# The routed expert part of a conv and mixture-of-experts block, in tiles of 128 tokens instead of 256

## The chip, the cores and the metric

The kernel runs on one NeuronCore of one Trainium2 chip. The metric is the device time in microseconds of that core, taken as the median of several runs; lower is better. One profiled execution of the same program gives the trace from which all rows below are read. In these rows PE is the matrix engine (TensorE), PEld its weight loads, PEldq its instruction sequencer, DVE is VectorE, ACT is ScalarE, POOL is GpSimd, and SP issues DMAs. PEclk is the share of TensorE's full clock that was granted: 1.00 is 2.4 GHz and 0.5 is 1.2 GHz.

## The reference

The input is 32 images of 128 channels with 32x32 pixels in float32. A dynamic depthwise 3x3 convolution runs first; after it every pixel is a token of 128 channels, 32768 in all, and each token goes through two of eight experts:

```python
x = x + _L0_conv_ref(_ln_c(x), ...)       # taps from per-channel mean and max, softmax over taps
t = _to_tokens(x)                         # (32768, 128)
# in _L0_ffn_ref, on xf = layernorm(t):
gate_logits = xf @ Wg + bg
top_w, top_i = jax.lax.top_k(gate_logits, 2)
top_w = jax.nn.softmax(top_w, axis=-1)
for e in range(8):
    h = gelu(xf @ W1[e] + b1[e])          # W1[e]: 128 x 512
    out = out + w_dense[:, e:e+1] * (h @ W2[e] + b2[e])   # W2[e]: 512 x 128
t = t + out
```

## The kernel before

The program has three stages, and every engine's order is written out by hand, with semaphores between the engines.

The **first stage** (0 to about 640 us) goes over pairs of images: layer norm, convolution, the gate, and the choice of the two experts. Its last step writes each token as a row of 133 numbers (128 channels, the two weights, the token's number, and the two numbers of its layer norm, `NMR` and `RSTD`) to DRAM by an indirect DMA of GpSimd (L439), into one of 28 lists: one list for each pair of experts. W1 and W2 are loaded into one buffer, `stage`, one after the other, and split into a high and a low float16 part (`split_weights`, L475 to L482 on ACT and L903 to L912 on DVE), which lie side by side in `wall`.

**Between the stages** DVE makes a table of the tiles (which rows, which two experts), and each list is filled up with empty rows to a whole tile (`pad`).

The **expert stage** goes over NT = 156 tiles of T = 256 rows (32768/256 = 128, and 28 for the lists' ends). For each tile SP loads the rows; ACT normalises them (`normalise`, L600); PE transposes them (`turn_rows`, L810) and ACT and DVE split the result into `xh` and `xl`. For both experts (side 0 and 1) `up` makes the hidden layer with 12 matmuls of 256 columns: four slices of the hidden layer times three products, high x high, high x low and low x high. ACT applies the gelu slice by slice, because each slice has its own bias column (L616). The result is split into `gh` and `gl`, and `down` takes the 128x128 blocks of these as the stationary operand and the weights as the moving one: `gh` against the high and the low weights at once (`both`, 256 columns, L841), `gl` against the high ones (128 columns, L842), and two matmuls for the bias (L845). DVE weighs the results (`combine`), GpSimd adds the two halves and the token's input (L447, L449) and scatters the rows to DRAM (L454).

Which expert a tile belongs to is known only at run time.
PE's order within a tile is `dstep`: up(j+1, side 0), turn_rows(j+2), down(j, side 0), experts(j+2), up(j+1, side 1), down(j, side 1). The body of its loop holds RING = 6 tiles.

The **last stage** reads the tokens back, transposes them and writes the images.

## Time and profile before

| | |
|---|---|
| median of 3 runs | 1923.3 us (1921.19 to 1933.44) |
| span of the profiled execution, first to last instruction | 1798.2 us |
| median less span | 125.1 us |
| first stage | 0 to about 640 us |
| PE without a matmul, between the stages | 38.0 us, up to 672.3 us |
| expert stage | about 674 to 1691 us |

The profiled execution's own device time is not listed, so the difference of 125.1 us is taken to the median of the runs. Busy shares on the page count matmuls, vector and scalar operations, but no register, branch or semaphore instruction.

### The profile page before, as it was taken

To read this page: it belongs to the slowest core of one execution; us is meant where nothing else is said; L and a number is where in the kernel's file an instruction comes from. 1 tells how busy PE (TensorE), PEld (TensorE's weight loads), DVE (VectorE), ACT (ScalarE), POOL (GpSimd) and SP (SyncE) were. 2 spreads that over 40 slices of the span, in tenths; PEclk is the share of its full clock that TensorE was granted. 3 is DMA by queue.
4 is the path that set the end of the run, shared out by engine and by line. 5 is a ranking of instruction groups with operands and counts; after the bars stand their busy time and mean duration, and the time that the engine had idled before them with its cause. 6 is when DMAs were issued, how large, how long until landed. Compare 5 with 4: busy or idle time off the path is not lost.

```text
span 1798.2 us, 45758 instructions
## 1 busy us (share of the span) xinstructions
PE 1536.5 (85%) x12335; PEld 1186.0 (66%) x12336; DVE 1396.4 (78%) x2440; ACT 1202.0 (67%) x2949; POOL 866.1 (48%) x905
## 2 busy tenths in 40 slices
PE   5889999999999519999999999999999999999665
PEld 2445555555555307878888778878777788878555
DVE  0468888788788737888888888888888888888644
ACT  3466667767666308878777887788777887888400
POOL 1003455355355464555555555555555555555500
PEclk8899999999998659999999999999999999999965
DMA  3211121121121061111111111111111111110099
GB/s 120 59 35 56 54 72 59 59 70 60 61 58 49 31 146 30 39 39 36 42 42 37 36 38 39 39 40 35 41 42 37 40 38 42 42 37 22 22 374 359
DMA packets 90626, 115.76 MB, mean 64 GB/s; under 512 B 15286, under 2 KB 71794, under 8 KB 90583
## 3 DMA queue, kind: packets, MB, share of 16 engines
q1 hardware_dynamic: 65784, 62.29, 12.2%
q0 software_dynamic: 18176, 34.27, 5.5%
q10 hardware_dynamic: 6624, 18.69, 2.8%
q8 instruction: 20, 0.33, 0.1%
q14 instruction: 22, 0.18, 0.0%
HBM read 60.22 MB, written 58.61 MB: 66 GB/s over the span
## 4 chain that ended last, share of the span: by engine, by line
issue 31%; POOL 28%; PE 24%; ACT 7%; DMA 4%; DVE 4%; POOLq 1%; SPq 0%; ACTq 0%; DVEq 0%
POOL token_out L454 12%; POOL yt L449 9%; PE psV L731 8%; POOL yt L447 6%; DMA ye<-token_out 4%; PE psR L703 3%; PE psV L691 3%; ACT spent L531 2%; PE psA L682 2%; PE psT L716 2%; PE psR L747 2%; PE psG L718 1%; POOL rows_by_pair L439 1%; DVE x L963 1%; ACT sq L508 1%
## 5 line engine op out<-in xcount | busy, mean ns | idle before, releaser
L1138 DVE TENSOR_TENSOR gl<-g,gh 128x1024 f16<-128x1024 f32 x312 | 438.1, 1404 | 70.5 <-ACT gh L624 65.2
L439 POOL DMA_INDIRECT rows_by_pair<-rows,idx x256 | 265.0, 1035 | 393.3 <-issue 245.4
L454 POOL DMA_INDIRECT token_out<-yt,rt x312 | 323.1, 1036 | 184.6 <-POOL yt L449 133.5
L616 ACT ACTIVATE g<-psV,b1col 128x256 f32<-128x256 f32 x624 | 244.4, 474 | 143.6 <-PE psV L825 143.6
L616 ACT ACTIVATE g<-psT,b1col 128x256 f32<-128x256 f32 x624 | 244.4, 474 | 53.4 <-PE psT L825 53.4
L731 PE MATMUL psV<-lp,diag 128*128 128x512 f32 x512 | 254.2, 626 | 24.8 <-ACT cv L524 14.6
L823 PE MATMUL psV<-xh,wall 128*128 128x256 f16 x624 | 171.9, 275 | 94.6 <-DVE xl L1128 53.8
L447 POOL TENSOR_TENSOR yt<-ya 128x256 f32<-128x256 f32 x156 | 112.9, 724 | 247.0 <-DVE ya L1150 246.9
L841 PE MATMUL psG<-wall,gh 128*128 x1248 | 222.7, 273 | 1.7 <-DVE ya L1146 1.4
L841 PE MATMUL psR<-wall,gh 128*128 x1248 | 222.7, 273 | 0.7 <-DVE ya L1150 0.7
L842 PE MATMUL psG<-wall,gl 128*128 x1248 | 214.3, 219 | 0.0
L842 PE MATMUL psR<-wall,gl 128*128 x1248 | 214.3, 219 | 0.0
L963 DVE SCALAR_TENSOR_TENSOR x<-lp,taps,x 128x1024 f32<-128x1024 f32 x160 | 205.3, 1283 | 3.5
L1136 DVE CAST gh<-g 128x1024 f16<-128x1024 f32 x156 | 145.8, 934 | 70.2 <-ACT g L616 70.1
L731 PEld LDWEIGHTS psV<-lp,diag 128*128 128x128 f32 x512 | 97.0, 199 | 152.6 <-issue 104.2
L823 PE MATMUL psT<-xh,wall 128*128 128x256 f16 x624 | 171.9, 275 | 0.1
L824 PE MATMUL psV<-xl,wall 128*128 128x256 f16 x624 | 170.7, 274 | 0.0
L825 PE MATMUL psV<-xh,wall 128*128 128x256 f16 x624 | 170.7, 274 | 0.0
L824 PE MATMUL psT<-xl,wall 128*128 128x256 f16 x624 | 170.7, 274 | 0.0
L825 PE MATMUL psT<-xh,wall 128*128 128x256 f16 x624 | 170.6, 273 | 0.0
L624 ACT ACTIVATE gh<-g 128x1024 f16<-128x1024 f32 x156 | 164.9, 1057 | 5.0
L600 ACT ACTIVATE xn<-rt 128x128 f32<-128x128 f32 x312 | 139.9, 514 | 42.1 <-DMA rt<-rows_by_pair 42.1
(187 smaller groups left out, 3254.9 us busy)
## 6 DMA issues: line engine op xcount, KB each, us to landing
rt<-rows_by_pair SPq DMA_DIRECT2D x156, 133.0 KB, 2.1
xb<-in_x_dram SPq DMA_DIRECT2D x32, 512.0 KB, 3.5
ye<-token_out SPq DMA_DIRECT2D x32, 512.0 KB, 9.1
out_dram<-oe ACTq DMA_DIRECT2D x32, 512.0 KB, 5.8
token_out<-yt,rt POOLq DMA_INDIRECT x312, 2.3
rows_by_pair<-rows,idx POOLq DMA_INDIRECT x256, 2.4
stage<-in_L_ffn_W_dram SPq DMA_DIRECT2D x1, 2048.0 KB, 12.3
rows_by_pair<-pad_rows SPq DMA_DIRECT2D x15, 133.0 KB, 5.2
```

The lines of the kernel that those rows point to most:

```text
L439: gp.indirect_dma_start(rows_dram, bass.IndirectOffsetOnAxis(ap=idx[p][:, b:b + 1].bitcast(U32), axis=0), rows[p][:, b, :], None).then_inc ...
L447: gp.tensor_tensor(yt[r][:, :, :], ya[r][:, :, 0:D], ya[r][:, :, D:2 * D], ALU.add).then_inc(ysum_done, 1)
L454: gp.indirect_dma_start(y_dram, bass.IndirectOffsetOnAxis(ap=rt[r][:, b, ID:ID + 1].bitcast(U32), axis=0), yt[r][:, b, :], None, bounds_ch ...
L616: last = sc_.activation(g[side][:, s * T:(s + 1) * T], hbank[side][:, s * T:(s + 1) * T], ACT.Gelu, bias=b1col[:, bass.ds(e * HS + s, 1)], ...
L731: ins = te.matmul(psConv.rearrange("p (h w) -> p h w", w=WW), diag[k][:, m, :], lp[j][:, y:y + HH // 2, dx:dx + WW], start=(m == 0), stop= ...
L823: te.matmul(out_, high, xh[q][:, :], start=True, stop=False)
L824: te.matmul(out_, high, xl[q][:, :], start=False, stop=False)
L825: last = te.matmul(out_, wall[:, bass.ds(w + (O_1L + s * P), P)], xh[q][:, :], start=False, stop=True)
L841: te.matmul(bank[:, 2 * b * D:2 * (b + 1) * D], gh[side][:, lhs], both, start=(s == 0 and b == 0), stop=False, skip_group_check=True)
L842: te.matmul(bank[:, 2 * b * D:(2 * b + 1) * D], gl[side][:, lhs], high, start=False, stop=False, skip_group_check=True)
L963: ins = v.scalar_tensor_tensor(out=img(x1[j]), in0=lp[j][:, dy:dy + HH, dx:dx + WW], scalar=taps[st_.slot(stage)][:, DVE_TAPS[m], k:k + 1] ...
L1138: v.tensor_tensor(gl[side][:, :], g[side][:, :], gh[side][:, :], ALU.subtract).then_inc(lo_done, 1)
```

## The change

- The tiles have T = 128 rows; NT becomes 32768/128 + 28 = 284. One `up` has 12 matmuls of 128 columns. The rings get 12 row buffers.
- PE works two tiles ahead: dstep(j) is up(j+2, 0), experts(j+3), turn_rows(j+4), down(j, 0), up(j+2, 1), down(j, 1). The hidden banks (`psA`, `psV`) and `g`, `gh`, `gl` are doubled by the tile's parity.
- `down` sums in 128 columns: `gh` x high, `gh` x low and `gl` x high are three matmuls of 128 columns into one place, and the bias is one matmul. `combine` makes the weighted sum and the token's input in two operations on DVE, with no addition on GpSimd.
- The bias b1 is folded into W1 between the stages: `NMR` is stored with 1 added, so that a normalised row adds up to D, and W1 less (its column sum less b1)/D is what is split. So W2 goes through `stage` first. ACT's gelu is one operation of 512 columns for each side.
- GpSimd normalises the rows, six tiles ahead, and scatters them.
- For PE the first 12 tiles and the last 20 are written out, and the loop between has 21 passes of 12 tiles.

```diff
-    T = 2 * P
-    TB = T // P
+    T = P
...
-    RING = 6
-    assert NT % RING == 0 and RING % 6 == 0
+    RING = 12
+    LOOPS = NT // RING - 1
+    AHEAD = 6
...
-        hbank = (psV, psT)
-        ybank = (psG, psR)
+        hbank = lambda side, r: (psA, psV)[side][:, H * (r % 2):H * (r % 2 + 1)]
+        xbank = lambda r: psT[:, 512 * (r % 2):512 * (r % 2) + P]
+        ybank = lambda side: (psG, psR)[side][:, 0:D]
...
+            sp.dma_start(stage_2, W2.rearrange("e (s p) d -> p e s d", p=P)).then_inc(s_stage, 16)
...
             sp.wait_ge(s_low, 1)
-            sp.dma_start(stage_2, W2.rearrange("e (s p) d -> p e s d", p=P)).then_inc(s_stage, 16)
+            sp.dma_start(stage_1, W1.rearrange("e d h -> d e h")).then_inc(s_stage, 16)
...
+            def normalise(j, r, t):
+                q = r % 4
+                pool.wait_ge(row_in[r % RING], 16 * (t + r // RING + 1))
+                if not isinstance(j, int) or j >= 4:
+                    pool.wait_ge(xT_ready, j - 3)
+                pool.sem_inc(row_seen, 1)
+                gp.tensor_scalar(xn[q][:, :], rt[r % RING][:, 0:D], rt[r % RING][:, RSTD:RSTD + 1], rt[r % RING][:, NMR:NMR + 1], ALU.mult, ALU.add).then_inc(xn_done, 1)
+            def scatter(j, r):
+                pool.reg_alu(tiles, tiles, 2, ALU.add)
+                pool.wait_ge(s_const, 3)
+                pool.wait_ge(ya_done, tiles)
+                gp.indirect_dma_start(y_dram, bass.IndirectOffsetOnAxis(ap=rt[r][:, ID:ID + 1].bitcast(U32), axis=0),
+                                      yt[r][:, :], None, bounds_check=NTOK - 1, oob_is_err=False).then_inc(y_out[r], 16)
+            for j in range(AHEAD):
...
+            for e in range(E):
+                act.wait_ge(s_shifted, e + 1)
+                sc_.activation(wall_e[:, e, O_1H:O_1L], stage_1[:, e, :], ACT.Copy, scale=WSCALE).then_inc(s_high, 1)
...
+            def gelu(j, side, r):
+                act.wait_ge(h_ready, 2 * j + side + 1)
                 if not isinstance(j, int) or j >= 2:
...
-            def gelu(j, side):
-                at = TW * j + T_EXP + side
-                e = act.value_load(tab[0:1, at:at + 1] if isinstance(j, int) else tab[0:1, bass.ds(at, 1)], min_val=0, max_val=E - 1)
-                act.wait_ge(h_ready, 2 * j + side + 1)
-                if not isinstance(j, int) or j >= 1:
-                    act.wait_ge(lo_done, 2 * j + side - 1)
-                for s in range(HS):
-                    last = sc_.activation(g[side][:, s * T:(s + 1) * T], hbank[side][:, s * T:(s + 1) * T], ACT.Gelu,
-                                          bias=b1col[:, bass.ds(e * HS + s, 1)], scale=1.0 / WSCALE)
-                last.then_inc(g_done, 1)
+                    act.wait_ge(lo_done, 2 * j + side - 3)
+                sc_.activation(g[side][r % 2][:, :], hbank(side, r), ACT.Gelu, scale=1.0 / WSCALE).then_inc(g_done, 1)
...
+            pe.wait_ge(s_stage, 32)
+            pe.wait_ge(s_b1, 1)
+            pe.wait_ge(cv_ready, 2 * NIMG)
+            pe.wait_ge(l_ready, NIMG)
+            pe.wait_ge(kept, NIMG)
+            pe.wait_ge(lg_ready, NU)
+            pe.wait_ge(idx_ready, NU)
+            for e in range(E):
+                te.matmul(shift_bank[e], ones[:, :], stage_1[:, e, :], start=True, stop=False)
+                te.matmul(shift_bank[e], ident[0:E, e:e + 1].broadcast_to([E, P]), b1n[:, :], start=False, stop=True).then_inc(s_shift, 1)
...
-                for b in range(TB):
-                    last = te.transpose(psA[:, 512 * (r % 2) + b * P:512 * (r % 2) + (b + 1) * P], xn[r % 2][:, b, :], ident[:, :])
-                last.then_inc(xT_ready, 1)
-            def up(j, side, q, o):
-                w = weights(o, side)
+                te.transpose(xbank(r), xn[r % 4][:, :], ident[:, :]).then_inc(xT_ready, 1)
...
+                    pe.wait_ge(g_done, 2 * j + side - 3)
+                for s in range(HS):
+                    out_ = hbank(side, r)[:, s * P:(s + 1) * P]
+                    high = wall[:, bass.ds(w + (O_1H + s * P), P)]
+                    te.matmul(out_, high, xh[r % 4][:, :], start=True, stop=False)
+                    te.matmul(out_, high, xl[r % 4][:, :], start=False, stop=False)
+                    last = te.matmul(out_, wall[:, bass.ds(w + (O_1L + s * P), P)], xh[r % 4][:, :], start=False, stop=True)
+                last.then_inc(h_ready, 1)
...
-                    pe.wait_ge(g_done, 2 * j + side - 1)
-                for s in range(HS):
-                    out_ = hbank[side][:, s * T:(s + 1) * T]
-                    high = wall[:, bass.ds(w + (O_1H + s * P), P)]
-                    te.matmul(out_, high, xh[q][:, :], start=True, stop=False)
-                    te.matmul(out_, high, xl[q][:, :], start=False, stop=False)
-                    last = te.matmul(out_, wall[:, bass.ds(w + (O_1L + s * P), P)], xh[q][:, :], start=False, stop=True)
-                last.then_inc(h_ready, 1)
-            def down(j, side, o):
-                w = weights(o, side)
+                    pe.wait_ge(ya_done, 2 * j + side - 1)
+                te.matmul(bank, bias_sel[:, :], wall[:, bass.ds(w + O_B2, D)], start=True, stop=False)
                 pe.wait_ge(lo_done, 2 * j + side + 1)
                 pe.wait_ge((hi0_done, hi1_done)[side], j + 1)
-                pe.wait_ge(ya_done, 2 * j + side + 1)
-                bank = ybank[side]
                 for s in range(HS):
-                    both = wall[:, bass.ds(w + (O_2 + 2 * s * D), 2 * D)]
                     high = wall[:, bass.ds(w + (O_2 + 2 * s * D), D)]
-                    for b in range(TB):
-                        lhs = slice(s * T + b * P, s * T + (b + 1) * P)
-                        te.matmul(bank[:, 2 * b * D:2 * (b + 1) * D], gh[side][:, lhs], both, start=(s == 0 and b == 0), stop=False, skip_group_check=True)
-                        te.matmul(bank[:, 2 * b * D:(2 * b + 1) * D], gl[side][:, lhs], high, start=False, stop=False, skip_group_check=True)
-                bias = wall[:, bass.ds(w + O_B2, D)]
-                for b in range(TB):
-                    last = te.matmul(bank[:, 2 * b * D:(2 * b + 1) * D], bias_sel[:, :], bias, start=False, stop=(b == TB - 1), skip_group_check=True)
+                    low = wall[:, bass.ds(w + (O_2 + (2 * s + 1) * D), D)]
+                    toks = slice(s * P, (s + 1) * P)
+                    te.matmul(bank, gh[side][r % 2][:, toks], high, start=False, stop=False)
+                    te.matmul(bank, gh[side][r % 2][:, toks], low, start=False, stop=False)
+                    last = te.matmul(bank, gl[side][r % 2][:, toks], high, start=False, stop=(s == HS - 1))
...
             def dstep(j, r):
-                more, q = not isinstance(j, int), r % 2
-                if more or j + 1 < NT:
-                    up(j + 1, 0, 1 - q, (r + 1) % 3)
-                if more or j + 2 < NT:
-                    turn_rows(j + 2, r)
-                down(j, 0, r % 3)
-                if more or j + 2 < NT:
-                    experts(j + 2, (r + 2) % 3)
-                if more or j + 1 < NT:
-                    up(j + 1, 1, 1 - q, (r + 1) % 3)
-                down(j, 1, r % 3)
-            with pe.Fori(0, NT // RING - 1, 1) as t:
+                last = isinstance(j, int)
+                if not last or j + 2 < NT:
+                    up(j + 2, 0, r + 2)
+                if not last or j + 3 < NT:
+                    experts(j + 3, r + 3)
+                if not last or j + 4 < NT:
+                    turn_rows(j + 4, r + 4)
+                down(j, 0, r)
+                if not last or j + 2 < NT:
+                    up(j + 2, 1, r + 2)
+                down(j, 1, r)
...
+            for e in range(E):
+                dve.wait_ge(s_shift, e + 1)
+                v.scalar_tensor_tensor(out=stage_1[:, e, :], in0=shift_bank[e], scalar=-1.0 / D, in1=stage_1[:, e, :], op0=ALU.mult, op1=ALU.add).then_inc(s_shifted, 1)
+            for e in range(E):
+                dve.wait_ge(s_high, 2 + e + 1)
+                v.scalar_tensor_tensor(out=wall_e[:, e, O_1L:O_2], in0=stage_1[:, e, :], scalar=WSCALE, in1=wall_e[:, e, O_1H:O_1L], op0=ALU.mult, op1=ALU.subtract).then_inc(s_low, 1)
...
+                if side == 0:
+                    v.scalar_tensor_tensor(out=ya[q][:, :], in0=ybank(0), scalar=rt[slot][:, W_LO:W_LO + 1], in1=rt[slot][:, 0:D],
+                                           op0=ALU.mult, op1=ALU.add).then_inc(ya_done, 1)
+                else:
+                    dve.wait_ge(ya_done, 2 * j + 1)
+                    v.scalar_tensor_tensor(out=yt[slot][:, :], in0=ybank(1), scalar=rt[slot][:, W_HI:W_HI + 1], in1=ya[q][:, :],
+                                           op0=ALU.mult, op1=ALU.add).then_inc(ya_done, 1)
```

The order of PE's instructions shows at two places what that makes of the instruction stream. The first is `down` of side 0, from its start to the second place of the weights. Before:

```order
L801 ISA
L841 ISA
L841 MATMUL psG<-wall,gh 128x256
L842 MATMUL psG<-wall,gl 128x128
L841 MATMUL psG<-wall,gh 128x256
L842 MATMUL psG<-wall,gl 128x128
L841 ISA
```

and in the changed kernel:

```order
L820 ISA
L851 ISA
L851 MATMUL psG<-wall,bias_sel 128x128
L852 REGISTER_ALU
L858 ISA
L858 MATMUL psG<-wall,gh 128x128
L859 ISA
L859 MATMUL psG<-wall,gh 128x128
L860 MATMUL psG<-wall,gl 128x128
L858 ISA
L858 MATMUL psG<-wall,gh 128x128
```

Before, four matmuls stand behind each address step (`L841 ISA`), with 256 and 128 columns in turn; now one stands behind the step of the high weights (`L858 ISA`) and two behind that of the low ones (`L859 ISA`), all of 128 columns.

The second place is `up` of side 0, from its start. Before:

```order
L819 ISA
L823 ISA
L823 MATMUL psV<-xh,wall 128x256
L824 MATMUL psV<-xl,wall 128x256
L825 ISA
L825 MATMUL psV<-xh,wall 128x256
L823 ISA
```

and in the changed kernel:

```order
L836 ISA
L840 ISA
L840 MATMUL psA<-xh,wall 128x128
L841 MATMUL psA<-xl,wall 128x128
L842 ISA
L842 MATMUL psA<-xh,wall 128x128
L840 ISA
```

Here the sequence has stayed: two matmuls behind one address step, one behind the next; only their columns went from 256 to 128.

For one tile in the loop's body the built program holds, before and now: matmuls 62 and 51; address steps and the like (`ISA`) 30.2 and 37.2; waits 5 and 4.9; register moves 1.8 and 2.8; register additions 1.2 and 4.2; loads from the table 1 and 1. (The waits and moves stand in no row of the order.) For one of the 32 tiles that are written out the changed program holds 32.4 `ISA`, 4.6 waits, 3.9 moves and no addition.

## Rows read from the trace of the kernel before

**Rows 1.** The page: its part 1 and two lines of its part 2.

```profile
PE 1536.5 (85%) x12335; PEld 1186.0 (66%) x12336; DVE 1396.4 (78%) x2440; ACT 1202.0 (67%) x2949; POOL 866.1 (48%) x905
...
PE   5889999999999519999999999999999999999665
...
PEclk8899999999998659999999999999999999999965
```

**Rows 2.** Table of windows, 1000 to 1600: from, to, length, busy by engine, clock, DMA.

```profile
1000.00:1600.00 600.00, 543.45 (x5700) 480.45 (x5701) 519.35 (x735) 479.88 (x1103) 348.99 (x368) 1.00 0.13 39
```

**Rows 3.** Line L798, and the waits, 1000 to 1600: total us, times, longest.

```profile
L798 PEldq TENSOR_LOAD <-tab x92: 532/537/541, 1002.4 to 1596.6; - x92
...
PEld psV L823 <- issue: 72.4, 92, 1.0
...
PE psV L823 <- DVE xl L1128: 33.4, 45, 0.8
```

**Rows 4.** Timeline of PE's weight loads behind a wait.

```profile
1202.84 0.10 PEld L823 LDWEIGHTS psV<-xh,wall 128*128 x1 [0.66 <-issue]
...
1202.97 0.10 PEld L825 LDWEIGHTS psV<-xh,wall 128*128 x1
1203.10 0.10 PEld L823 LDWEIGHTS psV<-xh,wall 128*128 x1
```

**Rows 5.** Lines one by one, PE's sequencer (PEldq), one tile: ns, first and last start.

```profile
L823 PEldq FUSED_REGOPS  x4: 42/46/51, 1202.7 to 1203.5; - x4
...
L825 PEldq FUSED_REGOPS  x4: 46/46/51, 1202.9 to 1203.6; - x4
...
L841 PEldq FUSED_REGOPS  x4: 46/46/46, 1204.2 to 1204.6; - x4
...
L808 PEldq EVENT_SEMAPHORE  x1: 51/51/51, 1203.8 to 1203.8; - x1
...
L798 PEldq TENSOR_LOAD <-tab x1: 536/536/536, 1204.9 to 1204.9; - x1
...
L801 PEldq MOVE  x2: 29/29/29, 1205.5 to 1207.6; - x2
...
L817 PEldq EVENT_SEMAPHORE  x1: 51/51/51, 1202.5 to 1202.5; - x1
```

**Rows 6.** Timeline of PE, 256 columns (L841) and 128 (L842, L845).

```profile
1201.91 0.27 PE L841 MATMUL psR<-wall,gh 128*128 x1
1202.02 0.22 PE L842 MATMUL psR<-wall,gl 128*128 x1
1202.08 0.28 PE L845 MATMUL psR<-wall,bias_sel 128*128 x2
```

**Rows 7.** The same at the tiles' start, 256 columns, clock 0.5.

```profile
674.70 0.42 PE L825 MATMUL psV<-xh,wall 128*128 128x256 f16 x1
674.91 0.42 PE L823 MATMUL psV<-xh,wall 128*128 128x256 f16 x1
```

**Rows 8.** Groups of instructions, 1000 to 1600: busy us, mean ns.

```profile
L1138 DVE TENSOR_TENSOR gl<-g,gh 128x1024 f16<-128x1024 f32 x184 | 258.8, 1407 | 41.2 <-ACT gh L624 38.0
...
L1136 DVE CAST gh<-g 128x1024 f16<-128x1024 f32 x92 | 86.1, 936 | 39.5 <-ACT g L616 39.5
...
L1150 DVE SCALAR_TENSOR_TENSOR ya<-psR,rt,ya 128x256 f32<-128x256 f32 x184 | 80.0, 476 | 0.0
...
L1128 DVE TENSOR_TENSOR xl<-psA,xh 128x256 f16<-128x256 f32 x91 | 37.3, 410 | 0.0
```

**Rows 9.** Lines of the weight split in the first stage.

```profile
L480 ACT ACTIVATE wall<-stage x8: 612/612/615, 88.1 to 91.7; 128x512 f16<-128x512 f32 x8
...
L911 DVE SCALAR_TENSOR_TENSOR wall<-stage,wall x8: 682/684/693, 92.4 to 96.6; 128x512 f16<-128x512 f32 x8
```

**Rows 10.** Line L439 from 640 on, and PE's timeline after its idle time.

```profile
L439 POOL DMA_INDIRECT rows_by_pair<-rows,idx x21: 963/967/971, 639.8 to 665.2; - x21
...
672.31 0.69 PE L810 MATMUL psA<-ident,xn 128*128 128x128 f32 x2 [38.02 <-ACT xn L600]
```

**Rows 11.** Timeline of PE in the first stage, clock 1.0: float32, 512 columns.

```profile
62.28 1.88 PE L731 MATMUL psV<-lp,diag 128*128 128x512 f32 x4
```

287 lines of the change are left out of this document (140 added, 147 removed).

## The prediction

> **What bounds the kernel now.** I read the page first. PE is busy for 85% of the span, the most of all engines, and its granted clock is full through the whole expert stage [rows 1]. That stage is more than half of the span, and the change rewrites it, so I asked for its steady part, 1000 to 1600 us. PE is busy there for 543 of 600 us, DVE for 519 and ACT for 480 [rows 2]. A busy share says little about what costs how much, so I worked out the period. The table is read once a tile, 92 times, from 1002.4 to 1596.6 us [rows 3]: 91 periods in 594.2 us, or **6.53 us for a tile of 256 rows**. 156 tiles make 1019 us.
>
> Next, the matmuls. A matmul of 256 columns holds the array for 0.11 us (1201.91 to 1202.02), one of 128 columns for 0.06 us (1202.02 to 1202.08), although each brings a weight load of its own [rows 6]. By 2.4 GHz it is 0.107 and 0.053; I take 0.109 and 0.055, between these and the rows. The tile has 24 + 16 matmuls of 256 columns, 16 + 4 of 128, and two transposes of 0.11: 4.36 + 1.10 + 0.22 = 5.7 us. The other 0.8 us is one gap in each tile ahead of `up`: 72.4 us in 92 gaps, of which part is put down to DVE's `xl` [rows 3].
>
> So far the array looks like the bound, with DVE close behind. But the weight loads after such a gap don't follow at the array's pace: of the steps L823, L825, L823 the loads start at 1202.84, 1202.97 and 1203.10, 0.13 us apart [rows 4]. Each of these three has an address step of its own in PE's instruction stream. The address steps themselves stand in the sequencer's lines, which no busy share counts. From 1202.7 (first L823) to 1203.6 (last L825) there are 7 intervals; L841's four steps lie in 1204.2 to 1204.6, three intervals with four matmuls in each [rows 5]. That is 0.13 us both times, whether one, two or four matmuls follow. Over the longest unbroken piece, from the first L823 at 1202.7 to the table's load at 1204.9, the sequencer takes 18 steps (8 of L823 and L825, one each of L805, L808, L801 and L834, 4 of L841, one of L845, and the two of L798): 2.2/18 = **0.122 us a step** [rows 5]. The load from the table takes 0.6 us to the next step (1204.9 to 1205.5). From the first wait of the tile (L817, 1202.5) to the last move (L801, 1207.6) the sequencer needs 5.1 us [rows 5]. Then it waits. It is a third engine near the bound: 5.1 of 6.53 us, hidden because each address step of `down` feeds four matmuls and each matmul is long.
>
> **The change, part by part.** I go by what PE's sequencer has to do, because the number of its steps goes with the number of tiles and not with the rows.
>
> *Smaller tiles, down product in 128 columns.* A tile of 128 rows has 24 matmuls in `up` and 26 in `down`, and one transpose: 50 x 0.055 + 0.11 = 2.86 us of array time, half of before. The steps are not halved: `up` has its 16 address steps as before, and `down` now has two for each slice where it had one, since high and low weights are fetched apart, so 16 and two for the bias. In the loop's body a tile has 7.0 `ISA` more than before, 3.0 additions and 1.0 move more, and its waits as before. Seven at 0.122 are 0.85 us; for the cheap kinds I take 0.09, from the move at 1205.5 which the next step follows by 1205.6 at the earliest. Four make 0.35. The sequencer then needs 5.1 + 0.85 + 0.35 = **6.3 us for each 128 rows**, over twice the array's time. It issues in order, so PE's array waits for it. In the 32 tiles that are written out it is 2.2 `ISA` and 2.1 moves more, 1.2 additions less: 5.1 + 0.27 + 0.08, about 5.4 us.
>
> The loop has 252 tiles: 252 x 6.3 = 1588 us. 32 x 5.4 = 173 us. Together 1761 us against 1019, or **+742 us**.
>
> The bounds: a tile has 49.1 steps beside the load. At 0.122 each they make 6.0, with the load 6.6 us, the upper end. At 0.110, which is less than any piece in [rows 5] gives, they make 5.4, with the load 6.0 us, the lower end. The bounds on the loop are +-76 us. A price below nothing, that is a gain from the steps, is excluded: they are more for each tile, and the tiles are more.
>
> *Two tiles ahead, doubled buffers.* They take away the gap of 0.8 us, since the operands of `up` are made a tile earlier. The sequencer has no slack for this to show: what is late next is the sequencer itself. Worth 0 here, 0.8 us a tile of 256 if the array were the bound.
>
> *ACT, DVE and GpSimd.* DVE's mean times for 1024 columns are 1407 and 936 ns, for the weighing 476 and for `xl` 410 [rows 8]. Halved they make, for a tile, 2 x 0.70 + 0.47 + 2 x 0.24 + 0.21 = 2.6 us; with the fixed part of an operation, as in 684 ns for 512 columns [rows 9] and at most 476 ns for a weighing, it is 3.1. Both are hidden under 6.3, and so are ACT (its gelus lose the bias's address steps) and GpSimd, with one scatter of 0.97 us [rows 10] and one operation for each tile. No row shows GpSimd's normalisation; from 0 to 3 us a tile it costs nothing.
>
> *W1 after W2.* The eight pieces of W2's split, 8 x 0.61 us on ACT and 8 x 0.68 us on DVE [rows 9], move from the second step to the first, where W1's stood: between 0 and -6 us, I take -3. The fold of b1 lies between the stages: 16 float32 products of 512 columns, at 1.88/4 = 0.47 us [rows 11] or twice that at the lower clock, 8 to 15 us, then 16 operations on DVE at 0.68 and 8 on ACT. PE is idle for 38.0 us there, up to 672.3, and GpSimd's last scatters run until 666 [rows 10]. That hides it: 0, or up to +10 if the three engines take turns worse than I think.
>
> **The sum.** The spans add up against 1923.3 us, the median, since what lies around the span (125.1 us) is not touched: 1923.3 + 742 - 3 = 2662, and I say **2660 us**.
>
> **A rule that speaks against this.** The rows give 0.12 us for a step of the sequencer. The Trainium skill (Runtime: NRT & Kernel Launch, Instruction fetch mechanics) states an issue floor of about 20 cycles for an instruction. By its clock of 1.2 GHz (TensorE: Matmul & The Clock Gate, Wait — 56ns, not 53.3ns?) that would be an estimated 17 ns, 50 steps would take under 1 us, and the steps would be hidden. By that rule the array stays the bound, which is the first rival below; the trace does not agree, with 0.122.
>
> **The rivals.** *The array stays the bound (faster).* Place: the address steps of a tile. If they ran beside the matmuls, the tile would go by the array's 2.86 us or DVE's 2.6 to 3.1; I take 3.0. 284 x 3.0 = 852, less 1019: 1923 - 167 - 3 = **1753 us**. It decides itself at a step price of (3.0 - 0.6)/49 = 0.05 us. Against it are all the intervals of [rows 4, 5]; for it, that an address step's own length is only 46 ns. Chance 0.06.
>
> *A cheaper step.* The steps may be held up by the array, which is full of long matmuls, and cost 0.08 to 0.11 us with short ones. Then a tile takes 4.5 to 6.0 us and the kernel **2180 to 2560 us**. Against it: the loads 0.13 apart came right behind the idle gap. 0.06.
>
> *The array falls to the lower clock too.* PE would be at work for under half of each tile. At clock 0.5 a matmul of 256 columns takes 0.21 us (674.70 to 674.91) [rows 7], so one of 128 takes 0.107, a group of twelve 1.28 us against 8 x 0.124 = 0.99 for its steps, and the tile 50 x 0.107 + 0.22 = 5.6, still under 6.3. The sequencer catches up between the groups, so I count 0; if it can't, 4 x 0.29 us a tile are 329 us more and the kernel takes **2990 us**. 0.07.
>
> **How the numbers follow.** The forecast has 0.81, the rivals 0.06, 0.06 and 0.07. The range 2540 to 2800 holds the forecast with its bounds (-76 to +76, +10, and some 45 us for stalls at the loop's 21 jumps back, 2 us each, the longest issue pause being 1.0 in [rows 3]) and leaves out the rivals. A measurement can tell 1% of this kernel from no change, so: faster by over 1% 0.06, within 1% 0.01, slower 0.93.
>
> **What would show it.** In the profile after, PE's sequencer lines should stand 0.12 us apart without a pause; the table's load should come every 6.3 us; PE's weight loads should be 0.12 us apart with short idle times put down to issue; DVE, ACT and GpSimd should be busy for under half of the stage, and PE's waits for them should be gone. The expert stage should last about 1760 us, and the first stage should be shorter by some 3 us. The prediction is wrong if the load comes every 3 us (the steps are hidden), or if DVE or ACT ends most of PE's idle time.

## The result and the profile after

The changed kernel takes 2822.1 us, the median of 4 runs (2805.6 to 2830.9); the kernel before took 1925.4 us beside it (1921.2 to 1933.4). The ratio is 1.463, with an interval of 1.457 to 1.470. All ratios leave out executions that took over 1.5% longer than the fastest of the same kernel. The direction and the cause were as predicted (2660 us, range 2540 to 2800); the time lies 22 us above the range, because three costs of the sequencer were put too low.

The profiled execution of the changed kernel took 2827.2 us and its span is 2825.5. Under 2 us lie around a span, and not the 125 us that the prediction assumed. The page of the changed kernel, its part 1, two lines of part 2 and one of part 3 (queue: packets, MB, share). Parts 1 and 2 of before stand in [rows 1]; its queue for instructions had 20 packets and 0.33 MB:

```profile
PE 2236.1 (79%) x17178; PEld 1508.3 (53%) x17179; DVE 1242.9 (44%) x2916; ACT 984.7 (35%) x2218; POOL 714.5 (25%) x849
...
PE   6988779787678887788777787777788777788874
...
PEclk7999888888589888998888888998889989889986
...
q8 instruction: 218, 3.57, 0.5%
```

The same stretch as in [rows 2], 1000 to 1600 us: PE's matmuls 482 us, DVE 220, ACT 182, GpSimd 135, at a clock of 0.89.

```profile
1000.00:1600.00 600.00, 481.69 (x4437) 347.22 (x4437) 220.38 (x522) 182.35 (x348) 135.04 (x175) 0.89 0.08 21
```

The table's loads in that stretch, as in [rows 3]: 87 from 1005.9 to 1599.9 are 594.0/86 = 6.91 us for a tile, and a tile has 128 rows now, so 13.8 us for the 256 rows that took 6.53.

```profile
L817 PEldq TENSOR_LOAD <-tab x87: 533/537/544, 1005.9 to 1599.9; - x87
```

The waits of the stretch (total us, times, longest): DVE and ACT wait for PE, GpSimd waits for DVE, and PE waits for no engine. Its own idle time stands as "issue", that is as time in which the profile shows nothing that it waited for.

```profile
POOL token_out L466 <- DVE yt L1172: 435.9, 83, 9.0
DVE ya L1168 <- PE psG L860: 230.4, 87, 6.3
ACT g L629 <- PE psV L842: 223.6, 87, 2.9
...
PEld psA L840 <- issue: 50.0, 84, 4.3
```

PE's sequencer in one tile, 1059.4 to 1065.9, as in [rows 5]. L840 and L842 are the address steps of the two `up` groups, L858 and L859 those of `down`:

```profile
L840 PEldq FUSED_REGOPS  x8: 42/46/51, 1060.9 to 1065.4; - x8
...
L842 PEldq FUSED_REGOPS  x8: 46/46/51, 1061.1 to 1065.7; - x8
...
L858 PEldq FUSED_REGOPS  x8: 46/46/46, 1059.6 to 1064.1; - x8
...
L859 PEldq FUSED_REGOPS  x8: 46/46/46, 1059.8 to 1064.2; - x8
```

The timeline of the weight loads shows those behind an address step 0.12 to 0.13 us apart, as in [rows 4]: 1202.72, 1202.85 and 1202.97. Over 1000 to 1600 us the step after an address step starts 0.124 us later in the median and 0.129 us later in the mean.

```profile
1202.72 0.10 PEld L858 LDWEIGHTS psG<-wall,gh 128*128 128x128 f16 x1 [0.20 <-issue]
1202.85 0.11 PEld L859 LDWEIGHTS psG<-wall,gh 128*128 128x128 f16 x1
...
1202.97 0.12 PEld L858 LDWEIGHTS psG<-wall,gh 128*128 128x128 f16 x1
```

What the prediction had too low is in three more rows of the changed kernel. Within one pass of the loop ten loads lie in 1042.2 to 1101.6, 6.60 us apart. In the last, written-out part sixteen lie in 2615.3 to 2706.1, 6.05 apart. And each jump back to the start of the loop (L885) holds the sequencer for 3.3 to 3.9 us:

```profile
L817 PEldq TENSOR_LOAD <-tab x10: 533/536/539, 1042.2 to 1101.6; - x10
...
L817 PEldq TENSOR_LOAD <-tab x16: 532/536/544, 2615.3 to 2706.1; - x16
...
L885 PEldq COMPARE_BRANCH  x7: 3331/3584/3867, 1030.8 to 1528.4; - x7
```

In the kernel before, the jump back of PE's loop takes 0.21 us:

```profile
L867 PEldq COMPARE_BRANCH  x15: 207/208/208, 1031.2 to 1579.9; - x15
```

The whole expert stage, first to last load of the table, is 790.5 to 2706.1 in the changed kernel and 665.6 to 1681.0 in the trace of before: 1915.6 us against 1015.4, or +900, beside a difference of the medians of +897. So the expert stage holds the whole loss, and nothing of weight is left for the other stages.

### The profile page after: what moved, and what is told of

The parts are those of the page before. It is cut to its first block, busy times and chain, and to the rows that moved or that the text cites. A ratio compares the mean times of both kernels' runs of the same rounds, so it can differ in the third digit from the quotient of the medians.

```text
span 2825.5 us, 63638 instructions
## 1 busy us (share of the span) xinstructions
PE 2236.1 (79%) x17178; PEld 1508.3 (53%) x17179; DVE 1242.9 (44%) x2916; ACT 984.7 (35%) x2218; POOL 714.5 (25%) x849
## 3 DMA queue, kind: packets, MB, share of 16 engines
q8 instruction: 218, 3.57, 0.5%
## 4 chain that ended last, share of the span: by engine, by line
PE 70%; issue 15%; DVE 4%; ACT 4%; DMA 3%; another core or an unknown queue 3%; SPq 1%; POOL 0%; ACTq 0%; POOLq 0%; DVEq 0%
PE psV L740 6%; PE psA L840 6%; PE psV L840 6%; PE psG L859 5%; PE psR L859 5%; PE psG L858 5%; PE psR L858 5%; PE psV L842 3%; PE psA L842 3%; PE psT L828 3%; PE psV L841 3%; PE psR L860 3%; DMA ye<-token_out 3%; PE psA L841 3%
## 5 line engine op out<-in xcount | busy, mean ns | idle before, releaser
L629 ACT ACTIVATE g<-psV 128x512 f32<-128x512 f32 x284 | 169.6, 597 | 718.2 <-PE psV L842 718.2
L1161 DVE TENSOR_TENSOR gl<-g,gh 128x512 f16<-128x512 f32 x568 | 390.2, 687 | 10.5 <-ACT gh L635 0.8
L840 PE MATMUL psA<-xh,wall 128*128 128x128 f16 x1136 | 273.2, 241 | 107.6 <-issue 83.8
L840 PE MATMUL psV<-xh,wall 128*128 128x128 f16 x1136 | 281.7, 248 | 29.6 <-issue 7.4
L858 PE MATMUL psR<-wall,gh 128*128 x1136 | 280.4, 248 | 18.9 <-issue 2.8
L858 PE MATMUL psG<-wall,gh 128*128 x1136 | 271.5, 239 | 25.1 <-issue 3.9
L842 PE MATMUL psV<-xh,wall 128*128 128x128 f16 x1136 | 285.2, 251 | 0.0
L859 PE MATMUL psR<-wall,gh 128*128 x1136 | 279.2, 247 | 0.9
L841 PE MATMUL psV<-xl,wall 128*128 128x128 f16 x1136 | 277.5, 244 | 0.0
L859 PE MATMUL psG<-wall,gh 128*128 x1136 | 272.1, 240 | 1.5
L842 PE MATMUL psA<-xh,wall 128*128 128x128 f16 x1136 | 272.3, 241 | 0.0
L841 PE MATMUL psA<-xl,wall 128*128 128x128 f16 x1136 | 266.3, 236 | 0.0
L635 ACT ACTIVATE gh<-g 128x512 f16<-128x512 f32 x284 | 178.9, 630 | 246.6 <-PE psR L860 246.6
L629 ACT ACTIVATE g<-psA 128x512 f32<-128x512 f32 x284 | 169.5, 597 | 261.2 <-PE psA L842 226.0
```

The source lines that it names most:

```text
L629: sc_.activation(g[side][r % 2][:, :], hbank(side, r), ACT.Gelu, scale=1.0 / WSCALE).then_inc(g_done, 1)
L635: sc_.activation(gh[1][r % 2][:, :], g[1][r % 2][:, :], ACT.Copy).then_inc(hi1_done, 1)
L840: te.matmul(out_, high, xh[r % 4][:, :], start=True, stop=False)
L841: te.matmul(out_, high, xl[r % 4][:, :], start=False, stop=False)
L842: last = te.matmul(out_, wall[:, bass.ds(w + (O_1L + s * P), P)], xh[r % 4][:, :], start=False, stop=True)
L858: te.matmul(bank, gh[side][r % 2][:, toks], high, start=False, stop=False)
```

## The experiments

Each was run beside the kernel before on the same chip, and ratios are to those runs. The times of before differ from chip to chip (1879 to 1925 us), so kernels of different groups are compared by their tiles. The period of a tile is always the first to the last load of the table in 1000 to 1600 us, by the number of intervals, unless another row is named.

**e0_before: the kernel before, unchanged.** The trace of before had its first tile at 666 us, that of the changed kernel at 791. This run asks whether the change or the execution does that.

> The kernel before, unchanged, profiled once more. The changed kernel's first stage took about 118 us longer than that of the first trace of before (first product of the expert stage at 792.8 against 674.3 us). Theory A (the first trace of before was taken in a quicker execution, and the change has no part in it): the span is about 1920 us here, and the expert stage starts near 790 us. Theory B (the change makes the first stage slower): the span is about 1798 us again and the stage starts near 674 us.

It took 1886.0 us, span 1884.3. The loads of its expert stage:

```profile
L798 PEldq TENSOR_LOAD <-tab x156: 532/536/721, 752.1 to 1765.7; - x156
```

The stage is as long as in the first trace (1013.6 us against 1015.4) and begins 86 us later, in the same program. The span lies between the two theories' and the start is nearer to A's. The first stage varies by itself; the trace of before that the prediction was read from was a quick execution, with a span of 1798.2 where the runs of before take 1862 to 1933. The changed kernel with a shorter PE loop (e1, the next run, on the same chip) reads its first table entry at 747.1 us, 5 us before this one. The late start is no cost of the change.

The fold between the stages can be seen the same way. From the end of the last rank product (the last matmul of the first stage) to the first turn of rows PE had 38.0 us in the first trace of before, but 54.2 in this one (701.9 to 756.1), 56.4 in the changed kernel (731.1 to 787.5) and 55.6 in the next run. So the fold costs 1 to 2 us.

**e1_pe4: the changed kernel, with a PE loop of 4 tiles instead of 12.** The steps of a tile are the same; only the loop's body is a third as long, and 276 instead of 252 tiles are in the loop.

```diff
-            for j in range(RING):
+            for j in range(4):
                 dstep(j, j)
-            with pe.Fori(1, LOOPS, 1) as t:
-                for r in range(RING):
-                    dstep(RING * t + r, r)
-            for j in range(RING * LOOPS, NT):
+            with pe.Fori(1, NT // 4 - 1, 1) as t:
+                for r in range(4):
+                    dstep(4 * t + r, r)
+            for j in range(NT - 4, NT):
                 dstep(j, j)
```

> The changed kernel with 4 instead of 12 tiles in the body of PE's loop (70 passes less one instead of 21); nothing else. In the changed kernel the jump back takes 3.3 to 3.9 us instead of 0.2, and the queue that fetches instructions has 218 packets instead of 20. Theory fetch (the body of 12 tiles no longer fits and is fetched again in each pass): no long jump any more, packets back to some 20 to 40, and about 20 x 3.8 = 76 us less, so near 2745 us. Rival (a jump costs 3.8 us of itself once the kernel has more code): 69 jumps, 180 us more, near 3000 us. The time of a tile between the jumps stays at 6.5 to 6.6 us, or falls to 6.3 if the fetching also delays the steps.

2704.7 us, ratio 1.442 (1.428 to 1.455). The lines of this kernel's jump and loads, 1000 to 1600:

```profile
L885 PEldq COMPARE_BRANCH  x23: 215/215/215, 1013.3 to 1587.0; - x23
...
L817 PEldq TENSOR_LOAD <-tab x92: 532/534/536, 1001.8 to 1595.2; - x92
```

And its page's instruction queue:

```profile
q8 instruction: 19, 0.31, 0.0%
```

The jump takes 0.2 us again and the instruction queue moves 0.31 MB where it moved 3.57. So the long jumps come from fetching: PE's body of 12 tiles, some 1830 instructions with the weight loads, was fetched anew in each pass. The rival is out: 69 jumps cost less than 20. A tile takes 593.4/91 = 6.52 us with its share of jumps. Its stage (747.1 to 2579.4, 1832.3 us) is 83 us shorter. The tiles without a jump take 6.38 to 6.44 us from turn to turn of the rows, against 6.60, and the step after an address step starts 0.125 us later in the mean, against 0.129. So fetching went with somewhat slower steps too.

**e2_static: the changed kernel without address steps.** The choice of the expert is left out: side 0 always takes expert 0 and side 1 expert 1, so the places in `wall` are constants, and the load from the table falls away too. Matmuls, waits, rows and the work of all other engines are the same. The results are not those of the block.

```diff
-                return pe.snap(off[r % 4][side], min_val=0, max_val=(E - 1) * EW)
+                return side * EW
```

> The changed kernel with the places of the weights fixed (experts 0 and 1 for every tile): it leaves out the choice of the expert, and with it the address steps and the load from the table on PE; matmuls, their sizes and the waits are the same. Theory steps (PE's sequencer is the bound, 0.124 us for each address step): the tile falls from 6.6 to between 2.9 and 3.2 us, and the kernel by 284 x 3.5 = 1000 us to about 1830 us; DVE's busy share in the stage rises above 80%. Rival (matmuls of 128 columns are slow of themselves, by their weight loads or the lower clock): the tile stays over 5 us and the kernel over 2400 us.

1679.8 us, ratio 0.896 (0.888 to 0.905). PE's turns of rows, one for each tile, by their line, 1000 to 1500:

```profile
L828 PEld LDWEIGHTS psT<-ident,xn x172: 140/140/140, 1001.9 to 1498.9; 128*128 128x128 f32 x172
```

The window of the same stretch:

```profile
1000.00:1500.00 500.00, 500.00 (x8777) 497.94 (x8775) 461.96 (x1032) 325.76 (x690) 293.62 (x345) 1.00 0.16 45
```

497.0/171 = **2.91 us for a tile**, with PE busy without a pause at the full clock; the prediction's array time was 2.86. The address steps, the register work around them, the load from the table and the fetching that went with them are worth 6.60 - 2.91 = 3.7 us of each tile, and nothing else in the change holds it up. The forecast of 1830 us was too high: it took off 3.5 us a tile where 3.7 went, and left out the jumps, which are short here (0.21 us). Halving the tiles is no loss in itself: 2 x 2.91 = 5.8 us for 256 rows is less than the 6.53 of before.

**e3_both: the changed kernel with the down product in 256 columns again.** Eight address steps fewer for each tile; DVE gets two additions more.

```diff
-                    te.matmul(bank, gh[side][r % 2][:, toks], high, start=False, stop=False)
-                    te.matmul(bank, gh[side][r % 2][:, toks], low, start=False, stop=False)
-                    last = te.matmul(bank, gl[side][r % 2][:, toks], high, start=False, stop=(s == HS - 1))
+                    te.matmul(bank, gh[side][r % 2][:, toks], both, start=(s == 0), stop=False, skip_group_check=True)
+                    te.matmul(bank[:, 0:D], gl[side][r % 2][:, toks], high, start=False, stop=False, skip_group_check=True)
```

> The changed kernel with the down product as before, high and low weights in one matmul of 256 columns (so one address step for each slice; the two halves are added by two more operations on DVE). PE's columns are the same, its address steps 8 fewer for each tile. Theory steps: 8 x 0.124 = 1.0 us less for each tile, 5.6 us, and 284 us less, near 2540 us. Rival (array or clock is the bound): no change within 1%, or a little slower by DVE's two operations.

2397.2 us, ratio 1.278 (1.263 to 1.293). 110 loads, 1002.1 to 1599.3:

```profile
L817 PEldq TENSOR_LOAD <-tab x110: 533/536/539, 1002.1 to 1599.3; - x110
```

597.2/109 = 5.48 us a tile, 1.12 less than the 6.60 of the changed kernel. This body of 12 tiles has some 1540 instructions and its jumps are short again (0.56 MB of instructions on the page), so the fetching went too, and with it the kernel came out below the expected 2540 us; against the tiles of e1 without a jump, 6.43 us, it is 0.95 us for eight steps, or **0.12 us a step**.

**e4_split8: the kernel before with eight address steps more.** The steps are added where the theory says that they are hidden.

```diff
-                        te.matmul(bank[:, 2 * b * D:2 * (b + 1) * D], gh[side][:, lhs], both, start=(s == 0 and b == 0), stop=False, skip_group_check=True)
+                        te.matmul(bank[:, 2 * b * D:(2 * b + 1) * D], gh[side][:, lhs], high, start=(s == 0 and b == 0), stop=False, skip_group_check=True)
...
+                    for b in range(TB):
+                        lhs = slice(s * T + b * P, s * T + (b + 1) * P)
+                        te.matmul(bank[:, (2 * b + 1) * D:2 * (b + 1) * D], gh[side][:, lhs], low, start=False, stop=False, skip_group_check=True)
```

> The kernel before with one edit: gh x high and gh x low are two matmuls of 128 columns instead of one of 256, the low ones behind an address step of their own. PE multiplies as many columns as before; a tile has 8 address steps more. Theory (PE's sequencer needs 0.122 us for each step, and before it needs 5.1 of a tile's 6.53 us): it needs 6.1 now, still under 6.53, so the tile stays at 6.5 to 6.7 us and the time within 2% of before. Rival (the time of a step is added to the matmuls' and hides behind nothing): 8 x 0.122 = 1.0 us on each of 156 tiles, 152 us, 8% slower. Rival (steps don't matter, only 128-column matmuls are slow in themselves): 16 more matmuls and weight loads in a tile for the same columns, each with some fixed 0.05 us: 0.8 us a tile, 125 us.

1957.6 us, ratio 1.021 (1.013 to 1.028). The loads:

```profile
L798 PEldq TENSOR_LOAD <-tab x89: 532/536/539, 999.9 to 1598.1; - x89
```

and, of the waits, PE's ahead of `up` (side 1 and side 0; total us, times, longest):

```profile
PEld psT L823 <- issue: 48.4, 89, 0.6
PEld psV L823 <- issue: 44.6, 88, 0.6
...
PE psV L823 <- ACT g L616: 29.4, 87, 0.4
```

598.2/88 = 6.80 us, against 6.54 in e0_before. Of the 1.0 us that eight steps cost at 0.12, about three quarters were hidden and 0.26 us showed. So "hides behind nothing" is out, and "6.5 to 6.7" was too good. The rival that short matmuls are slow of themselves isn't settled here; e2 and e5 speak against it. The waits point to the sequencer for the 0.26 us: ahead of `up` the weight loads wait on issue for 93.0 us, 1.06 a tile, where it was 72.4 in [rows 3], 0.79 a tile. The new wait is the one of side 1, right behind the load from the table. Why it shows there was not tried apart.

**e5_split22: the same matmuls, 14 steps more.** The two blocks of rows are done one after the other, and each works out its places again.

```diff
-                for s in range(HS):
-                    high = wall[:, bass.ds(w + (O_2 + 2 * s * D), D)]
-                    low = wall[:, bass.ds(w + (O_2 + (2 * s + 1) * D), D)]
-                    for b in range(TB):
+                for b in range(TB):
+                    w = weights(o, side)
+                    for s in range(HS):
+                        high = wall[:, bass.ds(w + (O_2 + 2 * s * D), D)]
+                        low = wall[:, bass.ds(w + (O_2 + (2 * s + 1) * D), D)]
```

> The matmuls of the last kernel (the same number, the same columns), in an order in which the two blocks of rows are done one after the other, so that every place in the weights is worked out twice: 22 address steps and 1.8 register additions more for each tile than before, 14 and 1.8 more than the last one. Theory: the sequencer needs 5.1 + 22 x 0.122 + 0.2 = 8.0 us, now more than the array's 5.7 and everything else, so a tile takes 7.8 to 8.2 us and the kernel 200 to 260 us more than before (10 to 14% slower). Rival (the array or another engine sets the tile; steps are hidden as long as there is as much to multiply): no change against the last kernel.

2212.5 us, ratio 1.151 (1.144 to 1.157).

```profile
L798 PEldq TENSOR_LOAD <-tab x72: 533/536/548, 1003.4 to 1596.6; - x72
```

593.2/71 = 8.35 us, and the kernel takes 296 us more than before, where 200 to 260 were expected: the theory's 8.0 us was again too low. From the 5.1 us that the prediction gave the sequencer it would be 3.25 us for 22 steps and 1.8 additions, 0.14 a step. But in this trace the step after an address step starts 0.124 us later in the median and 0.128 in the mean; so it is the 5.1 that is too low, and not the price. Against e4 the matmuls are the same, of the same columns, in another order: with 14 address steps and 1.8 additions more the tile is 1.55 us longer and the kernel 13% slower (2212.5 against 1957.6).

**e6_fold256: the rest of the change, in tiles of 256 rows.** b1 folded, one gelu for each side, GpSimd normalises; ACT makes both `gh`, in two buffers.

```diff
+                for b in range(TB):
+                    last = gp.tensor_scalar(xn[q][:, b, :], rt[r][:, b, 0:D], rt[r][:, b, RSTD:RSTD + 1], rt[r][:, b, NMR:NMR + 1], ALU.mult, ALU.add)
...
-                for s in range(HS):
-                    last = sc_.activation(g[side][:, s * T:(s + 1) * T], hbank[side][:, s * T:(s + 1) * T], ACT.Gelu,
-                                          bias=b1col[:, bass.ds(e * HS + s, 1)], scale=1.0 / WSCALE)
+                sc_.activation(g[side][:, :], hbank[side][:, :], ACT.Gelu, scale=1.0 / WSCALE).then_inc(g_done, 1)
...
+                sc_.activation(gh[side][q][:, :], g[side][:, :], ACT.Copy).then_inc((hi0_done, hi1_done)[side], 1)
```

> The kernel before, still in tiles of 256 rows and with gh against high and low weights in 256 columns, with what the change has besides: b1 folded into W1 so that a gelu is one operation of 1024 columns, GpSimd normalises the rows; and ACT now makes both gh, with two buffers each, DVE only the low parts and the weighing. PE's instructions are those of before. Theory: PE's array needs 5.7 us a tile, its sequencer 5.1, ACT 2 x 1.1 + 2 x 1.06 + 0.4 = 4.7, DVE 2 x 1.4 + 4 x 0.47 + 0.41 = 5.1, GpSimd 3.8 + 2 x 0.44 = 4.7. What made PE wait in each tile (0.8 us) was DVE and ACT, so the tile goes from 6.53 to 5.7 to 5.9 us: 156 x 0.7 = 110 us less than before, 5 to 7% faster. Rival: the wait ahead of the first matmul of a tile comes from the sequencer or from the turn of the rows through PE, ACT and DVE, and stays: 6.4 to 6.5 us a tile, no change.

1977.2 us, ratio 1.030 (1.025 to 1.035): a miss. A tile takes 6.94 us (87 loads, 1000.7 to 1597.6) where 5.7 to 5.9 were expected, and the wait has a name:

```profile
PEld psA L828 <- POOL xn L454: 94.9, 43, 2.9
```

PE waits for GpSimd's normalised rows in every other tile.

**e7_fold4: the same, GpSimd normalises four tiles ahead.**

```diff
-                q = r % 2
+                q = r % 3
...
-                if not isinstance(j, int) or j + 3 < NT:
-                    normalise(j + 3, (r + 3) % RING, t + (r + 3) // RING)
+                if not isinstance(j, int) or j + 4 < NT:
+                    normalise(j + 4, (r + 4) % RING, t + (r + 4) // RING)
```

> The last version in tiles of 256 rows (b1 folded, GpSimd normalises, ACT makes both gh) lost time because PE waited for the normalised rows in every other tile (up to 2.9 us, 94.9 us in 600). Here GpSimd normalises four tiles ahead instead of three, in three buffers; nothing else is changed. Theory: that wait was all that held the tile at 6.9 us; without it the array's 5.7 us is the bound: 5.8 to 6.0 us a tile, 80 to 110 us less than before (4 to 6% faster). Rival (GpSimd itself is too slow: it is busy for 5.3 us a tile and issues two scatters, and its waits add up): the tile stays at 6.5 us or more and PE still waits for GpSimd's rows.

1962.8 us, ratio 1.027 (1.019 to 1.036); 6.83 us a tile (594.5/87). The theory fell and the rival held. GpSimd's groups, 1000 to 1600:

```profile
L468 POOL DMA_INDIRECT token_out<-yt,rt x176 | 226.4, 1286 | 104.5 <-POOL yt L463 75.8 <-issue 28.7
L454 POOL TENSOR_SCALAR xn<-rt 128x128 f32<-128x128 f32 x176 | 108.9, 630 | 2.7
L463 POOL TENSOR_TENSOR yt<-yt,rt 128x256 f32<-128x256 f32 x88 | 85.9, 976 | 6.9
L461 POOL TENSOR_TENSOR yt<-ya 128x256 f32<-128x256 f32 x88 | 68.4, 778 | 0.0
```

It is idle for 114.1 us, almost all of it its own: 75.8 us between the addition and the scatter that reads it, 28.7 of issue. The busy times with these fill the stretch. GpSimd is the bound here, and working further ahead cannot help it. The expectation of e6 had put its busy time at 4.7 us a tile, where it is 5.5 here, and had left out 104.5/88 = 1.2 us a tile of its own waits ahead of the scatters.

**e8_fold: the kernel before with b1 folded, and nothing else.** ACT normalises as before.

> The kernel before with one part of the change alone: b1 is folded into W1 between the stages, so a gelu is one operation of 1024 columns instead of four of 256, and ACT reads no expert's number. GpSimd, DVE, PE's stream and the tiles are those of before. Theory: PE's sequencer (5.1 us) and array (5.7) are not changed; ACT falls from about 5.2 to 4.3 us a tile, but a gelu now starts when all four slices of the hidden layer are there, so its result comes no earlier than before. DVE (5.65 us a tile and its waits for ACT, 0.4 us twice) stays close behind, so the tile stays within 6.3 to 6.6 us and the time within 2% of before; the fold between the stages costs at most 10 us. Rival (ACT's eight short gelus held the chain of the tile): 6.0 us a tile, 80 us less.

1895.1 us, ratio 0.989 (0.985 to 0.994); 6.43 us a tile (93 loads, 1003.6 to 1595.2). ACT lost a fifth of its work and the kernel 1%, since PE still waits for DVE:

```profile
PE psV L830 <- DVE xl L1139: 48.1, 94, 0.8
```

**e9_round: e8 with both `gh` on ACT, and DVE in another order.**

```diff
-                    sc_.activation(gh[1][:, :], g[1][:, :], ACT.Copy).then_inc(hi1_done, 1)
+                sc_.activation(gh[side][q][:, :], g[side][:, :], ACT.Copy).then_inc((hi0_done, hi1_done)[side], 1)
...
-                    v.tensor_copy(gh[0][:, :], g[0][:, :]).then_inc(hi0_done, 1)
...
-                if more or j + 1 < NT:
-                    split(j + 1, 0)
                 if more or j + 2 < NT:
                     low(j + 2, r % 2)
                 combine(j, 0, r)
+                if more or j + 1 < NT:
+                    split(j + 1, 0, 1 - r % 2)
+                combine(j, 1, r)
                 if more or j + 1 < NT:
-                    split(j + 1, 1)
-                combine(j, 1, r)
+                    split(j + 1, 1, 1 - r % 2)
```

> The version with b1 folded (tiles of 256 rows, ACT normalises as before) with one thing more: ACT makes gh of both sides, in two buffers each, where DVE made that of side 0, and DVE takes xl and the weighing of side 0 ahead of the split. GpSimd has its old work. Theory: in that version the array waits 0.5 us a tile for DVE's xl, and DVE is busy for 5.6 us of 6.43. DVE falls to 4.7, ACT rises from 4.1 to 5.2, PE's sequencer stays at 5.1, so the array's 5.7 is the bound: 5.75 to 6.0 us a tile, 85 to 120 us less than before (4 to 6% faster). Rival (the chain from up over gelu, gh and gl to down is what holds the tile, and with ACT doing two long operations in a row it gets no shorter): 6.3 to 6.5 us a tile, 0 to 2% faster.

1755.7 us, median of 6 (1739.8 to 1768.3), against 1878.9: ratio **0.930** (0.925 to 0.935), somewhat better than the 4 to 6% expected. The window, 1000 to 1600:

```profile
1000.00:1600.00 600.00, 600.00 (x6528) 552.33 (x6527) 483.16 (x736) 525.70 (x738) 466.66 (x420) 1.00 0.15 44
```

The loads:

```profile
L813 PEldq TENSOR_LOAD <-tab x106: 532/537/682, 1000.2 to 1598.8; - x106
```

598.6/105 = 5.70 us a tile, PE busy for 600 of 600 us. That is the array time of 5.7 us which the prediction had worked out for the kernel before, and the sequencer's steps, those of before, stay hidden. This version beats both kernels. Which of its two edits over e8, `gh` on ACT or DVE's order, gave how much was not tried apart. Against e7 it differs only in who normalises the rows (and in how far ahead): 6.83 us a tile with GpSimd, 5.70 with ACT.

## Where the prediction was right, and which steps of it failed

**The bound.** The prediction said that PE's sequencer is a third engine near the bound (5.1 of 6.53 us a tile), hidden only because each step feeds long or many matmuls. e2, e3 and e5 show it from three sides: with the steps gone 2.91 us a tile, with eight fewer 5.48, and in the kernel before with 22 more 8.35. The array's time was right to 2% (2.86 against 2.91; 5.7 against 5.70 in e9).

**The steps for each tile.** "6.3 us" in the loop is the first step that failed, by its size: a tile took 6.60, the upper end of the bounds given. The price of a step was right (0.122 predicted; 0.124 in the median here, 0.12 by e3). The 5.1 us that the new steps were added to was too low: it was read in one tile, from the start of its first step to the start of its last. The 38.2 steps that the program has for a tile make 5.3 us at 0.122, with the load's 0.6. In e1, without the fetching, a tile takes 6.43 us, so 0.1 us of the missing 0.3 is this low start, and 0.2 goes with fetching beside the steps, which no term had. 252 x 0.3 = 76 us.

**The written-out tiles.** "5.4 us" was 6.05. The count of 32.4 `ISA` was a mean over a piece of program whose last two tiles have no `up`; a full tile has 34 (32 in `up` and `down`, two for the bias), which is 0.2 us, and the low start of 5.1 is 0.1 to 0.2 more. The last 0.3 us stays open. It may be fetching, since each instruction of written-out code runs only once. Against the long body as its cause speaks e3, whose jumps are short: its last tiles take 4.99 us, and their steps at the median times make 4.7. The 32 tiles cost 21 us more than predicted.

**The jumps.** They stood only in the range, at 2 us each. They take 3.3 to 3.9 us, and the tile with one takes 10.2 to 10.7 us from turn to turn of the rows instead of 6.6. There are 20 of them (the loop has 21 passes). A pass takes 83.0 us in the median, 3.8 more than 12 x 6.60, and 20 of these are 77 us. e1 shows their cause and takes them away. It is the term without which the range would have held: the forecast had no row for a long body, and bounded the jump by the longest pause in a kernel whose body is short.

76 + 21 + 77 = 174 us make 1761 us into 1935. The measured stage is some 19 us shorter, because it is counted from first to last load, one period less than there are tiles, and the first three loads stand together ahead of the first tile.

**What lies around the span.** The 125.1 us were not around the span at all: in e0 1886.0 us go with a span of 1884.3, so the first profiled execution, with its span of 1798.2, must have been a quick one. The sum added its difference to the median, and the expert stage is as long in both traces (1015.4 and 1013.6 us), so this was harmless. That was luck, since no row had shown it.

**The hidden terms** held. DVE was busy for 220.4/87 = 2.53 us a tile (2.6 to 3.1 predicted) and ACT and DVE wait for PE. The fold cost 1 to 2 us by the runs above, and the waits of two tiles' lead were worth nothing where the sequencer is the bound. That the first stage gets 3 us shorter can't be told: it varies by tens.

**The rivals.** "The array stays the bound" was wrong, but e2 shows what it would have been: 0.896 of before (the prediction said 1753 of 1923 us, 0.912). The Trainium skill (Runtime: NRT & Kernel Launch, Instruction fetch mechanics) puts an issue floor of about 20 cycles on an instruction; the address steps of this trace stand 0.124 us apart, some seven times the estimated 17 ns. A floor is only a least time, so the trace doesn't contradict it, but it was no price to count with. "A cheaper step" was wrong, with steps as dear beside short matmuls as beside long ones; its upper end, 6.0 us a tile, is 2605 us by the sum that gives its lower end, and not 2560. "The lower clock" came true as a fact and not as a cost. Two neighbouring windows of the changed kernel, one at clock 1.00 and one at 0.72:

```profile
1052.00:1058.00 6.00, 4.92 (x48) 3.31 (x46) 2.01 (x5) 2.10 (x4) 1.54 (x2) 1.00 0.09 25
1058.00:1064.00 6.00, 5.02 (x47) 4.06 (x46) 2.53 (x6) 2.10 (x4) 1.49 (x2) 0.72 0.05 11
```

48 and 47 matmuls in 6 us: the matmuls get longer and the pace stays, since the sequencer sets it. The first tile behind a jump shows it down to the lowest clock, 0.50; in both of these passes it takes 6.59 to 6.60 us from load to load:

```profile
1201.30:1207.90 6.60, 5.88 (x56) 4.56 (x53) 2.25 (x6) 2.10 (x4) 0.00 (x0) 0.71 0.05 10
...
1450.50:1457.10 6.60, 6.17 (x54) 5.08 (x52) 1.93 (x6) 2.10 (x4) 0.00 (x0) 0.50 0.04 9
```

With the steps gone (e2) the clock is at 1.00 from 1000 to 1500 us.

## What to carry to other kernels

Where operands are addressed by run-time registers, count the sequencer's steps for each unit of work as an engine of its own, at 0.12 to 0.13 us each here, and count them from the program rather than from one tile of a trace: smaller tiles and narrower matmuls multiply them, and no busy share shows them. Keep them under the array's time by making each step feed several matmuls, and look at the jump back and at the instruction queue's bytes when a loop's body grows. Read the engine that makes the bound engine wait, with its own waits counted in (GpSimd's 1.2 us here), before work is moved to it: with b1 folded and `gh` on ACT the kernel was 7% faster than before while ACT normalised the rows (e9), and 3% slower once GpSimd did (e7).

## What the runs showed of the hardware

**Instruction fetch.** PE's loop bodies of some 980, 1220, 1320 and 1540 instructions (before, e4, e5, e3; weight loads counted) jump back in 0.2 us; one of some 1830 takes 3.3 to 3.9 us and moves instructions in each pass. The Trainium skill (Runtime: NRT & Kernel Launch, Instruction fetch mechanics) says that PE holds 2048 instructions and that a jump to a place outside the current window costs a fetch stall. The second half agrees with e1. By the first, one could expect a body of 1830 to stay, and it didn't; why not, no run shows. Where between 1540 and 1830 it turns was not tried.

**DVE and GpSimd take longer side by side.** In the timeline of before, DVE's split takes 1.23 us in one half of a tile and 1.59 in the other, when GpSimd adds beside it. So it is in all of 1000 to 1600 us: the 92 splits with an addition beside them take 1.58 to 1.60 us, the 92 without 1.22 to 1.23.

```profile
1203.82 1.23 DVE L1138 TENSOR_TENSOR gl<-g,gh 128x1024 f16<-128x1024 f32 x1 [0.53 <-ACT gh L624]
...
1206.71 1.01 POOL L449 TENSOR_TENSOR yt<-yt,rt 128x256 f32<-128x256 f32 x1
1207.22 1.59 DVE L1138 TENSOR_TENSOR gl<-g,gh 128x1024 f16<-128x1024 f32 x1
```

GpSimd's first addition took 0.72 us in every tile of before, beside DVE's cast (L1136), which has one input; in e9, where DVE's operations lie otherwise, the same addition takes 0.72 to 1.77. The two rows, of before and of e9, 1000 to 1600:

```profile
L447 POOL TENSOR_TENSOR yt<-ya x92: 717/720/747, 1003.3 to 1597.6; 128x256 f32<-128x256 f32 x92
```

```profile
L450 POOL TENSOR_TENSOR yt<-ya x105: 720/993/1767, 1000.2 to 1597.6; 128x256 f32<-128x256 f32 x105
```

The Trainium skill (SBUF — State Buffer, SBUF: two separate sides) speaks of a port pair that GpSimd and DVE operations with two inputs hold in turns; the rows agree that two such operations are slower together, though both get longer here, also the addition that began first (1206.71, with 1.01 us where it takes 0.68 in e9 beside other work), and no run isolates it. GpSimd is busy for 467 of 600 us in e9. With its idle time ahead of the scatters (89.8 us for its own addition, 34.1 of issue) it is all but the next bound:

```profile
POOL token_out L457 <- POOL yt L452: 89.8, 105, 0.9
...
POOL token_out L457 <- issue: 34.1, 105, 1.4
```
